# Layer 2's FFN: gates of 12 of 16 chunks spread over the partitions by DMA instead of by matmul

## What is computed

```python
sel_logits = jnp.einsum('nd,ed->ne', xt, expert_sel)
gates = jax.nn.sigmoid(sel_logits)
sel_val, sel_idx = jax.lax.top_k(gates, N_HEADS)              # N_HEADS = 4
gate_full = jnp.zeros_like(gates).at[jnp.arange(N)[:, None], sel_idx].set(sel_val)
scores = jax.nn.relu(jnp.einsum('nd,edf->nef', xt, keys))     # 32 experts x 64 keys
scores = scores * gate_full[:, :, None]
out = jnp.einsum('nef,efv->nv', scores, values)
```

## Time and profile before

| | us |
|---|---|
| median of 3 runs | 2154.56 (2151.91 to 2160.38) |
| the profiled execution | 2148.3 |
| its span | 2146.5 |
| TensorE busy | 1702.9 (79%) |
| VectorE busy | 1370.1 (64%) |
| ScalarE busy | 908.6 (42%) |
| GpSimd busy | 796.0 (37%) |
| mean busy share of 16 DMA engines | 16.8% for SyncE's queue |

### The profile page before, as it was taken

The page is one execution under the profiler, slowest core; times in us unless marked ns, Lnnn a source line. Parts: engine busy times, 40 slices in busy tenths (PEclk is TensorE's granted clock), DMA queues, the critical chain, the costliest instruction groups (busy, mean ns, idle before and its releaser), DMA issues.

```text
span 2146.5 us, 28517 instructions
## 1 busy us (share of the span) xinstructions
PE 1702.9 (79%) x10489; PEld 1016.6 (47%) x10530; DVE 1370.1 (64%) x3068; ACT 908.6 (42%) x1591; POOL 796.0 (37%) x662
## 2 busy tenths in 40 slices
PE   7798688677889879877678876986678897888667
PEld 4476565212457666423236565651125575664113
DVE  4534356989663445697964534569986534467996
ACT  3443234454444333454444432345444443335554
POOL 2411012877232111384732302137862311114792
PEclk9968798877997999878798998996689979899679
DMA  5003501120000341212100123121200003402120
GB/s 193 1 1 92 148 14 58 47 84 31 6 5 1 87 137 30 63 41 73 41 1 11 30 84 111 31 66 44 85 24 6 1 1 110 129 14 84 47 77 10
DMA packets 96588, 113.64 MB, mean 53 GB/s; under 512 B 7616, under 2 KB 70848, under 8 KB 96192
## 3 DMA queue, kind: packets, MB, share of 16 engines
q1 hardware_dynamic: 94400, 107.63, 16.8%
q0 software_dynamic: 2048, 4.20, 0.7%
HBM read 88.86 MB, written 22.94 MB: 52 GB/s over the span
## 4 chain that ended last, share of the span: by engine, by line
PE 51%; DVE 21%; issue 8%; ACT 6%; POOL 6%; DMA 5%; SPq 4%; DVEq 0%; ACTq 0%; POOLq 0%
PE P L228 9%; DVE M L1990 7%; PE P L1615 5%; POOL M L2060 3%; PE P L955 3%; PE P L1823 3%; PE P L1198 2%; SPq L1438 2%; DMA W<-in_e 2%; PE P L1203 2%; PE P L1214 2%; SPq L1439 1%; PE P L390 1%; DVE M L201 1%; PE P L217 1%
## 5 line engine op out<-in xcount | busy, mean ns | idle before, releaser
L1990 DVE TENSOR_TENSOR_SCAN M<-P,M 128x512 f32<-128x512 f32 x384 | 447.8, 1206 | 23.7 <-ACT P L1904 12.2
L1823 PE MATMUL P<-M,wt 32*32 32x512 f32 x3072 | 272.8, 778 | 158.5 <-DVE M L1990 112.7
L1904 ACT ACTIVATE P<-M,negA 128x512 f32<-128x512 f32 x384 | 264.3, 690 | 249.7 <-DVE M L1990 227.2
L228 PEld LDWEIGHTS P<-wt,M 128*128 128x128 f32 x2176 | 279.3, 195 | 98.4 <-issue 35.7
L228 PE MATMUL P<-wt,M 128*128 128x128 f32 x2176 | 293.6, 281 | 13.4 <-DVE M L1320 2.3
L2060 POOL TENSOR_TENSOR M<-M 128x512 f32<-128x512 f32 x192 | 243.5, 1300 | 162.0 <-DMA M<-du 96.1
L2060 POOL TENSOR_TENSOR M<-W,M 128x512 f32<-128x512 f32 x192 | 243.7, 1301 | 50.0 <-PE P L1823 49.9
L1823 PEld LDWEIGHTS P<-M,wt 32*32 32x32 f32 x3072 | 39.3, 116 | 342.5 <-DVE M L1990 250.1
L209 POOL TENSOR_TENSOR st<-st,wt 128x4 f32<-128x4 f32 x64 | 84.2, 1315 | 286.1 <-DVE st L192 285.2
L1615 PE MATMUL P<-M,wt 128*128 128x512 f32 x256 | 141.4, 635 | 11.9 <-ACT M L1673 6.0
L1712 DVE TENSOR_TENSOR M<-M,P 128x512 f32<-128x512 f32 x128 | 87.4, 684 | 86.5 <-PE P L1623 65.3
(11 more groups left out here) (334 smaller groups left out, 3293.0 us busy)
## 6 DMA issues: line engine op xcount, KB each, us to landing
W<-in_e SPq DMA_DIRECT2D x152, 192.0 KB
M<-dt SPq DMA_DIRECT2D x64, 256.0 KB, 5.0
M<-xs SPq DMA_DIRECT2D x32, 256.0 KB, 4.7
ys<-M SPq DMA_DIRECT2D x32, 256.0 KB, 2.3
M<-du SPq DMA_DIRECT2D x32, 256.0 KB, 4.9
W<-du SPq DMA_DIRECT2D x32, 256.0 KB, 5.7
W<-xh SPq DMA_DIRECT2D x16, 256.0 KB
xs<-zero SPq DMA_DIRECT2D x2, 1216.0 KB, 10.6
```

Of the source, the lines that this page charges most:

```text
L228: m = e.matmul(out[:, tok(j)], h[:, tok(j)], wgt, start=first and j == 0, stop=last, skip_group_check=True)
L1823: m = e.matmul(t["sums"][i // 2][to:to + 32, :], part("WC", c)[r, r], scan[r, :], start=c == 0, stop=c == 5, tile_position=(32 * i, to))
L1904: e.activation(t["aa"][n % 2][:, :], t["dtr"][i][:, :], EXP, scale=negA[:, c:c + 1]).then_inc(ACT.s, ACT.mark(b, "a3", "aa", n))
L1990: e.tensor_tensor_scan(bb[:, :], t["aa"][n % 2][:, :], bb[:, :], 0.0, MUL, ADD).then_inc(DVE.s, DVE.mark(b, "a3", "scan", n))
```

## The change

`F2_NEAR = 4`: chunks 0 to 3 stay as they are. For chunks 4 to 15 of each block:
- the finished fp32 gates (line 1698) are also turned on TensorE, four transposes into 32 partitions of `P[3]`, copied by ScalarE to `T[22]`, and written by SyncE to a DRAM tensor `g_d` of 32 x 512;
- when that write has landed, SyncE issues 12 DMAs, one a chunk, each of which reads the two rows of the chunk's experts 64 times into a free tile `T[9]` to `T[20]`. Three DMAs share a semaphore, so the tiles come free for use in groups of three chunks: 4 to 6, 7 to 9, 10 to 12, 13 to 15;
- there is no gate matmul and no positive part on ScalarE. VectorE takes the scores from PSUM and does both in one `scalar_tensor_tensor`, max with 0 and product with the tile. The scores go round three banks, `P[1]`, `P[3]` and `P[2]`;
- the four order strings that give turns to the lanes on TensorE, ScalarE, VectorE and GpSimd are new ones, and SyncE's too, over the whole program.

```diff
+        g_d = [nc.dram_tensor(f"g{s}", [32, T], f32, kind="Internal").ap() for s in range(2)]
+        g_out = [sem(f"g_out{s}") for s in range(2)]
+        gates_in = [[sem(f"gates_in{s}_{k}") for k in range(4)] for s in range(2)]
...
+        F2_NEAR = 4
+
+        def f2_key_bank(L, c):
+            return L.P[2] if c < F2_NEAR else L.P[(1, 3, 2)[(c - F2_NEAR) % 3]]
+
+        def f2_gates(L, c):
+            return L.T[9 + c - F2_NEAR]
...
             def key(c):
                 yield
-                if c:
+                if 0 < c < F2_NEAR:
                     w.wait_ge(ACT.s, ACT.of(b, "f2", "relu", c - 1))
-                e.matmul(P[2][:, :], part("f2k", c), xn[:, :], start=True, stop=True).then_inc(
+                elif c == F2_NEAR + 2:
+                    w.wait_ge(ACT.s, ACT.of(b, "f2", "relu", F2_NEAR - 1))
+                elif c in (F2_NEAR, F2_NEAR + 1):
+                    w.wait_ge(DVE.s, DVE.of(b, "f2", "h", c - 2))
+                elif c:
+                    w.wait_ge(DVE.s, DVE.of(b, "f2", "h", c - 3))
+                e.matmul(f2_key_bank(L, c)[:, :], part("f2k", c), xn[:, :], start=True, stop=True).then_inc(
                     PE.s, PE.mark(b, "f2", "key", c))
...
             yield
+            w.wait_ge(DVE.s, DVE.of(b, "f2", "g"))
+            for j in range(4):
+                m = e.transpose(P[3][0:32, tok(j)], L.sm[:, 8 + 32 * j:40 + 32 * j], ident)
+            m.then_inc(PE.s, PE.mark(b, "f2", "g32"))
+            yield
             w.wait_ge(DVE.s, DVE.of(b, "f2", "g3"))
...
+            w.wait_ge(PE.s, PE.of(b, "f2", "g32"))
+            e.activation(T_[22][0:32, :], P[3][0:32, :], COPY).then_inc(ACT.s, ACT.mark(b, "f2", "g32"))
...
-                e.tensor_tensor(hg[c % 2][:, :], rl[c % 4][:, :], P[(1, 3)[c % 2]][:, :], MUL).then_inc(
-                    DVE.s, DVE.mark(b, "f2", "h", c))
+                if c < F2_NEAR:
+                    w.wait_ge(PE.s, PE.of(b, "f2", "gate", c))
+                    w.wait_ge(ACT.s, ACT.of(b, "f2", "relu", c))
+                    e.tensor_tensor(hg[c % 2][:, :], rl[c % 4][:, :], P[(1, 3)[c % 2]][:, :], MUL).then_inc(
+                        DVE.s, DVE.mark(b, "f2", "h", c))
+                else:
+                    w.wait_ge(PE.s, PE.of(b, "f2", "key", c))
+                    w.wait_ge(gates_in[b % 2][(c - F2_NEAR) // 3], 48 * (b // 2 + 1))
+                    e.scalar_tensor_tensor(hg[c % 2][:, :], f2_key_bank(L, c)[:, :], 0.0, f2_gates(L, c), MAX, MUL).then_inc(
+                        DVE.s, DVE.mark(b, "f2", "h", c))
...
+        def sp_ffn2(e, w, b):
+            L, s = lanes[b % 2], b % 2
+            yield
+            w.wait_ge(ACT.s, ACT.of(b, "f2", "g32"))
+            e.dma_start(g_d[s], L.T[22][0:32, :]).then_inc(g_out[s], 16)
+            yield
+            w.wait_ge(g_out[s], 16 * (b // 2 + 1))
+            for c in range(F2_NEAR, 16):
+                e.dma_start(f2_gates(L, c), g_d[s][2 * c:2 * c + 2, :].unsqueeze(1).to_broadcast([2, 64, T])).then_inc(
+                    gates_in[s][(c - F2_NEAR) // 3], 16)
...
-            "sync": (sp_attn0, sp_ffn1, sp_attn3, sp_ffn3),
+            "sync": (sp_attn0, sp_ffn1, sp_ffn2, sp_attn3, sp_ffn3),
```

More of the change, by code:

```diff
@@ L1620, in gate @@
                     w.wait_ge(DVE.s, DVE.of("c", "sel32"))
+                if c == 1:
+                    w.wait_ge(ACT.s, ACT.of(b, "f2", "g32"))
                 if c > 1:
@@ L1643, in pe_ffn2 @@
             for c in range(16):
-                if c < 13:
+                if c == F2_NEAR - 2:
+                    yield from key(c + 2)
+                if c == F2_NEAR - 1:
+                    yield from key(c + 2)
+                if c < F2_NEAR - 3 or F2_NEAR - 1 <= c < 13:
                     yield from key(c + 3)
-                if c < 15:
+                if c + 1 < F2_NEAR:
                     yield
@@ L1671, in act_ffn2 @@
             yield
+            w.wait_ge(PE.s, PE.of(b, "f2", "g32"))
+            e.activation(T_[22][0:32, :], P[3][0:32, :], COPY).then_inc(ACT.s, ACT.mark(b, "f2", "g32"))
+            yield
             w.wait_ge(PE.s, PE.of(b, "f2", "gT"))
             e.activation(gT, P[1][:, :], COPY).then_inc(ACT.s, ACT.mark(b, "f2", "gT"))
-            for c in range(16):
-                if c < 13:
-                    yield from key(c + 3)
+            for c in range(3, F2_NEAR):
+                yield from key(c)
         def dve_ffn2(e, w, b):
@@ L1707, in gate @@
                 yield
-                w.wait_ge(PE.s, PE.of(b, "f2", "gate", c))
-                w.wait_ge(ACT.s, ACT.of(b, "f2", "relu", c))
                 if c > 1:
                     w.wait_ge(PE.s, PE.of(b, "f2", "out", c - 2))
-                e.tensor_tensor(hg[c % 2][:, :], rl[c % 4][:, :], P[(1, 3)[c % 2]][:, :], MUL).then_inc(
-                    DVE.s, DVE.mark(b, "f2", "h", c))
+                if c < F2_NEAR:
[8 more added lines that the diff above has]
+                        DVE.s, DVE.mark(b, "f2", "h", c))
             yield from gate(0)
@@ new lines, in program @@
+            "tensor": (2075,
+                "000000200b8836dff826ffffea8fe100000424e03cb7fffe1ed83f11a80ff8787c5ffc03c1e00000003cf03c8fc393bffffd"
+                "ddb078c7025205c1ac2649fffc3c80900319be4007b7ff934fdfffea1fc2000024f00f26cffff7bfc3343f73607747f87871"
+                "7807e8bc21ed042000004ffe8fec9ffc001e2b80017fc19c2615ff0e4003cb079be4003daffe4d3f7fffa87f080000212701"
+                "d57f0c69fded4a630f87f0f1bffe01e0f01c8000000f3c1ff0eb3bffffffb43ca583fef8004b85aff8407b81b80826c8001c"
+                "157f87d97ffff6861e988000092190f793187fc46ec61fc3e1fcdbff878783c04d00000079e07c3f5cefffffff60f2c60fff"
+                "fbfffc000f707afc200"),
@@ new lines, in program @@
+            "scalar": (1428,
+                "000080ccccc73ff72fb00211200dfff7d9fa81e225fe039c01ffee0840000080aaee02a43fbfd6ff696abff26000bfc037e6"
+                "7d9fda7d8011501137ff7ff65b8a3f1c65c0bcf05af00000000008095fc03bffffd6fee962fe40e027f803de67d9fda7d801"
+                "089006fd37f7ae631c4bf80e70c9ffba18800020953e8147ffff7fc016ff75e00e0e3cc0003de0df7f74a9ac0112403f4beb"
+                "b31fc63a7dc0e7095ff7438400020953f0147ffffffff7ff200e3fe00"),
+            "vector": (2303,
+                "0000003ffc98502de000000079fd006f3fffbfe3ff0300e0000007bfd4fff5ffce7806018140029f40bad3bc042d57c197ea"
+                "54cb3a548aa01eaa0120de7aaadd5682dfffffc6125d074207ffff27c85bf800000146fd80de7fff7fd7ff038001b505f483"
+                "f7dbdf3d7999807ec43a0aeda40f57c00082952b08bff4808000112a80f55013afffaadd5682dfff55503035c81efffff87c"
+                "85bf800000146fd80de7fff7fcffc0c0001002200fff5ff5ffebe82a0180c050006f55d701fa457fc197fd54beaa4aa01eaa"
+                "00fffffbff8008ceaab7d540afe2a82df0000fff87a06ff80000001b00fe9ffeffbfbff41028000041103ffe7f5ffffc09b0"
+                "180a024007eabaa81b6a1ffc197fd597d2a4aa01eaa00fffffffffefffe6280792aafe001f80"),
@@ L2237, in program @@
             "gpsimd": (610,
-                "03f0c7c1f24a0000002490000fffcfff7fff8fcff0c7c1f0e800002000000071fffffecf6ffffc9f1ee1f0f0000920040000"
-                "0fffff9fff7ffe0ff0c7c1f0f00002002240000ffffffffffff34"),
-            "sync": (191,
-                "424cfc003ffcc027fc003fedc00ffc003ffc804ff8007ffa"),
+                "03f0c7c1f0e800022240000283fffdbff7fffe33f0c7d0f5304800000120000fffffcffefffe0ff0c7c1f0cc0024840001ff"
+                "ffeffc021ffcfd89f057c1f0ca0024900001ffffbfff7fefc00c8"),
@@ L2242, in program @@
+            "sync": (207,
+                "4093fca003ffcccccccc003ffcc027fa6021ffc801fecc043ffc"),
         }
```

20 lines of the change are left out of this document (2 added, 18 removed).

## The result

| | before | after |
|---|---|---|
| median, us | 2153.96 | 2523.12 (2519.47 to 2526.82, 4 runs) |
| the profiled execution's span | 2146.5 | 2517.7 |
| mean granted TensorE clock in it | 0.851 | 0.803 |

The ratio is 1.172 [1.169, 1.175], so the kernel became 369 us slower; the forecast was 2466, with 2360 to 2540 around it, so the measured time lies inside the range, 17 us from its upper end. The new lines to follow: f2's gates on 1732, the key matmul on 1636, the products on 1747 (old form, chunks 0 to 3) and 1752 (new form), the gate write on 2228, the spreads on 2232, f2's x on 1761, and the first scan step on 2100.

A forecast was written before the change was run, and what follows sets the result against it. TensorE was taken to bound f2, with slow two-engine spreads deciding the change: pairs +87, +56, +82 and +86 sum to +311 us, on the median of 2154.6 giving 2466 us, range 2390 to 2540, 8 in 10 within 2360 to 2540.

The forecast's parts named there:

- The price of a spread: Each new gate DMA in layer 2's FFN runs on two DMA engines at 50 GB/s: 5.24 us, 62.9 us a block.
- G: In each f2 block, finished gates to last gate landed: 1.7 to issue, 2.0 write, 2.0 and 62.9 for spreads, 68.6 us.
- the stretch: A's finished gates to A's next layer's first scan step, four pairs, 324.2 us before; forecast to grow by 311 us.
- credits: Fewer of B's chunks left behind the first scan step, subtracted from the pairs' sums: 7 us in pair 0.
- outside the stretches: The rest of the program, other layers in new order: taken as unchanged, with some 20 us either way.
- Pair 2: Blocks 2 and 3: B's gate write and spreads queue behind A's, 64.9 us later; 141.0 us against 84.5, left at +56.
- My remark: Without ring order holding later DMAs behind the two loaded engines, the sum falls by at most 7.5 us a pair.
- A step that was wrong without harm: On SyncE's queue, issuing a block's 12 spreads needs only 12 x 0.6 = 7 us.
- Sixteen engines: Rival: spreads served as line 2076's, 12 in 15 us, all hidden; 9 to 21 us faster, 2140 us; chance 0.13.
- Half hidden: Rival: slow gates, but B's wait runs beside A's layer 3 and scan; +180, 2335 us; chance 0.09.
- Two engines under load: Rival: two engines at 36 GB/s, 7.2 us a spread, +187, 2653 us; counted as part of the forecast's 0.78.
- The marks: Expected profile signs: spreads issued within 8 us, DMA share 0.12 to 0.15, VectorE waiting in three-chunk groups, scans as before.

The follow-up runs named there:

- e1: The changed kernel with keys and values of chunks 4 to 15 laid out so each spread reads [64, 2, T]; ratio 0.999 to the kernel before.
- e5: The changed kernel with each gate row written to DRAM eight times, so that a spread reads [16, 8, T]; ratio 1.014 to the kernel before.
- e9: e1 with the gate transposes and their copy in blocks 5 and 7 some steps earlier on TensorE and ScalarE; ratio 1.000 to the kernel before.
- e10: The same kernel as e1, nothing changed, run again beside e9 on one chip; ratio 1.001 to the kernel before.

## Why the prediction was right, point by point

**The price of a spread** carried the forecast and held: 5.24 us and 49 to 50 GB/s from line 2094's rows, 5.3 us and 49 to 51 GB/s measured. e1 changes the outermost size of the pattern (with the layout of the keys that this needs, which by e5 is not what the 369 us hang on), moves the same bytes, and the whole 369 us go. This is what turns the reading of the share (0.13 of 16 engines is two) from an argument into something shown, and the Trainium skill's rule (DMA: Bandwidth & Descriptors, "Rules for kernel authors") holds for 2, 4, 16 and 64 outermost.

**The terms of the sum,** predicted and measured in us:

| term | predicted | pair 0 | pair 2 | pair 4 | pair 6 |
|---|---|---|---|---|---|
| A's gates to its last gate landed (G) | 68.6 | 70.9 | 74.4 | 75.9 | 76.3 |
| from there to A's x | 5.0; 8.5 in pairs 4, 6 | 12.2 | | 7.9 | 3.9 |
| A's x to B's gates | 17.5 | 13.1 | | 18.0 | 18.6 |
| B's gates to its last gate landed | 68.6; 64.9 after A's in pair 2 | 68.2 | 65.2 | 76.7 | 74.6 |
| from there to the first scan step | 7.5 | 7.1 | 7.4 | 6.6 | 6.4 |
| the stretch | 167.2, 141.0, 170.7, 170.7 | 171.5 | 147.0 | 185.1 | 179.8 |

The sum came out at +371.2 in the profiled execution where +311 was forecast. The mechanism was right and the sum 16% too small. The 60 us are three sizes, and within the first lies a misreading:
- 34 us in the terms. Seven G's are 37 us too long together, the other rows 3 too short. G put 1.7 us from the gates to the write's issue; it was 2.7 and 1.6 in the first pair, 5.4 in block 2, and 5.5, 10.2, 5.5 and 8.0 in the last two pairs. These are 27 of the 37 us. Most of the others are the spreads of A's blocks: from the first issue to the last gate they took 66.4 to 67.3 us, where B's took the 64.9 that I had put. I let the four transposes cost their own time. What they cost is their place: on TensorE they stand behind the other lane's matmuls in a fixed order, and everything that follows is one chain from them. e9 shows this: with the transposes some steps earlier, block 5's write goes out 5.1 us after its gates instead of 10.3.
- Within these 34 us one term was misread, and the net hides it. I took the order on VectorE in pair 0 to be the same as before, but the order strings put the end of B's attention ahead of A's x there, where it had stood behind. So from the last gate to A's x it took 12.2 us and not 5.0 (VectorE waits for a matmul of B's attention in it), and from A's x to B's gates 13.1 and not 17.5.
- 14 us of credits (7, 0, 2 and 4 us for fewer chunks behind the scan, and rounding) that did not show. No run tested why.
- 12 us outside the stretches, the new orders of the other layers, which I had priced at nothing with 20 us either way. It lies within what single executions with the new orders differ by there: e1 and e10, one kernel, are 7 us above before and 1 us below it. So no cause can be given for these 12 us.

**Pair 2** went as told, by two causes where I had named one. SyncE's queue:

```profile
944.95 0.33 SPq L2228 DMA_DIRECT2D g<-M  x1
947.49 52.26 SPq L2232 DMA_DIRECT2D M<-g  x12
999.80 5.19 SPq L2228 DMA_DIRECT2D g<-M  x1
1014.12 9.69 SPq L2232 DMA_DIRECT2D M<-g  x4
```

B's gate write is issued 49 us after B's gates, because SyncE is still issuing A's spreads. Then it takes 14.3 us to land where the median is 1.6, and it lands at 1014.1, as A's last spread does (1013.9). This is the ring order of the Trainium skill's "Queues, rings and completion order" in one row: a DMA that uses all 16 engines waits behind those that load two. My remark that the sum would lose at most 7.5 us a pair without it was tried by no run.

**A step that was wrong without harm.** I had SyncE issue 12 spreads in 7 us, from the earlier trace rows, and then be free. It needed 51. In this kernel the error may well have been without effect on the sum, since by the ring order A's dt and du would have had to wait for the spreads in either case. That is argued from pair 2's write, and no run tried it. That the error did not hurt the sum is luck, since I had not worked it out.

**The rivals.** *Sixteen engines* forecast 2140 us if the pattern were served as line 2076's. It was not, but e1 makes its condition true and gives 2155: the premise "all is hidden" held in the waits (2.7 us for gates in all), yet the 21 us do not show. In pairs 4 and 6 they go between A's x and B's gates, where the new order puts B's attention. *Half hidden* needed B's f2 to run beside A's scan. From B's gates to B's x there were 95.7, 134.8, 95.3 and 92.8 us, and nearly all of it was on the path: A's scan started only 75.2, 136.1, 83.3 and 81.0 us after B's gates, since dt and du stood behind B's spreads. *Two engines under load* would have had spreads of 7.2 us; they took 5.3.

**The marks.** As told: share 0.13 and 50 GB/s, groups of three 16 us apart, VectorE's waits over 200 us (283), ScalarE's instructions down by 88, which is 96 positive parts less and 8 copies more. Not as told: the twelve issued within 8 us, and "line 1823 and the scans as before". That line (now 1863) is busy 286.4 us and not 272.8 and waits 190.9 us and not 158.5, as in every kernel here with the new orders.

## What to carry to other kernels

Before spreading rows by DMA, read the outermost size of the pattern, and look for a DMA of the same pattern in the old trace. Its share of 16 engines, in a window where it runs alone, is the price, whatever the total DMA load (10% here) says of room. If the size is small, reorder what lies on the partitions so that the repeats come outermost; this cost nothing here but a permutation of the weights on the host. A slow DMA holds the issuing engine and the loaded DMA engines for all that stands behind, so look at whose turn comes next in that queue even when nobody waits for the data.

And do not take a shorter chunk for a shorter program. Here the chunk became 0.22 us shorter, and 96 of them changed the whole by nothing measurable. With the new orders other waits took the place of the gate matmuls, and with the old ones key matmuls and dt came late. No kernel here combined sixteen-engine spreads with orders that avoid both, so what the shorter chunk is worth at best is open.
